# Last layer of a two-layer network on one core: biases inside the expert loop, rows added back on POOL, the end block by block

## The reference, cut to what matters

```python
x = x + _L1_ffn_ref(_layernorm(x, axis=-1), ...)

def _L1_ffn_ref(hidden_states, Wr, W1, b1, Wo, bo, gamma, beta):
    x = hidden_states.reshape(-1, H)
    expert_idx = jnp.argmax(jax.nn.softmax(x @ Wr.T, axis=-1), axis=-1)
    inter = jnp.zeros((x.shape[0], W1.shape[2]), dtype=x.dtype)
    for e in range(E):
        mask = (expert_idx == e)[:, None].astype(x.dtype)
        inter = inter + mask * jax.nn.gelu(x @ W1[e] + b1[e], approximate=False)
    y = inter @ Wo + bo + x
    mu = jnp.mean(y, axis=-1, keepdims=True)
    var = jnp.mean(jnp.square(y - mu), axis=-1, keepdims=True)
    return (y - mu) * jax.lax.rsqrt(var + LN_EPS) * gamma + beta
```

## Time and profile before

| | |
|---|---|
| median of 3 runs | 999.55 us (998.99 to 1000.77) |
| the profiled execution, its own time | 1001.5 us |
| its span, first to last instruction | 1000.2 us |
| busy over the span | PE 78%, DVE 68%, ACT 52%, POOL 24% |
| last part (from the barrier near 868 us) | 132 us |
| expert loop, first gather to last down copy | 896.4 to 973.6 us |
| behind the loop | 973.6 to 1000.2 us |

### The profile page before, as it was taken

The page is one execution under the profiler, slowest core; times in us unless marked ns, Lnnn a source line. Parts: engine busy times, 40 slices in busy tenths (PEclk is TensorE's granted clock), DMA queues, the critical chain, the costliest instruction groups (busy, mean ns, idle before and its releaser), DMA issues. The chain is left out here.

```text
span 1000.2 us, 17637 instructions
## 1 busy us (share of the span) xinstructions
PE 775.2 (78%) x6736; PEld 339.7 (34%) x6736; DVE 678.7 (68%) x1293; ACT 517.2 (52%) x994; POOL 237.2 (24%) x287
## 2 busy tenths in 40 slices
PE   4747998887623999970889899999999999628770
PEld 2315224663312666650411122222222222415650
DVE  5647997447676444438598899999999981573345
ACT  2563543265621333320516788888888887303342
POOL 0001101033205566634372200000000000026650
PEclk9967999998855999995956999999999999958995
DMA  3080000000070111114577221303300000051112
GB/s 105 0 168 3 2 1 13 5 4 1 0 291 31 40 43 43 41 31 143 175 156 185 77 48 30 75 6 72 76 2 3 2 2 2 17 224 43 42 33 87
DMA packets 40218, 58.06 MB, mean 58 GB/s; under 512 B 12025, under 2 KB 27393, under 8 KB 39369
## 3 DMA queue, kind: packets, MB, share of 16 engines
q1 hardware_dynamic: 36168, 48.82, 18.2%
q0 software_dynamic: 3968, 8.13, 3.1%
HBM read 37.99 MB, written 14.75 MB: 53 GB/s over the span
## 5 line engine op out<-in xcount | busy, mean ns | idle before, releaser
L867 DVE TENSOR_REDUCE arena<-psum 128x1 f32<-128x1024 f32 x256 | 301.0, 1216 | 26.5 <-PE psum L749 23.7
L963 ACT ACTIVATE arena<-psum 128x512 f32<-128x512 f32 x512 | 266.9, 604 | 53.1 <-PE psum L763 53.1
L749 PE MATMUL psum<-arena 56*128 56x512 bf16 x512 | 181.4, 413 | 8.4 <-DVE arena L867 4.7
L763 PE MATMUL psum<-arena 59*128 59x512 bf16 x512 | 157.8, 389 | 8.9 <-ACT arena L963 6.1
L774 PE MATMUL psum<-arena 128*32 128x512 f32 x1024 | 137.9, 611 | 8.7 <-issue 8.7
L763 PEld LDWEIGHTS psum<-arena 59*128 59x128 bf16 x512 | 37.8, 94 | 171.2 <-ACT arena L963 147.2
L437 POOL DMA_INDIRECT rows_y<-arena x62 | 62.8, 1012 | 64.0 <-DVE arena L392 61.3
L352 PEld LDWEIGHTS psum<-arena 128*128 128x128 f32 x496 | 62.9, 193 | 38.9 <-issue 25.5
L352 PE MATMUL psum<-arena 128*128 (+1 forms) x496 | 67.3, 279 | 10.7 <-ACT arena L416 10.7
L343 PE MATMUL psum<-arena 128*128 x124 | 68.0, 632 | 2.3 <-DVE arena L377 2.1
L432 POOL DMA_INDIRECT arena<-rows_x,arena x62 | 61.3, 989 | 34.7 <-issue 16.4
(11 more groups left out here) (292 smaller groups left out, 1138.7 us busy)
## 6 DMA issues: line engine op xcount, KB each, us to landing
arena<-scr_k SPq DMA_DIRECT2D x15, 448.0 KB
arena<-scr_q SPq DMA_DIRECT2D x15, 448.0 KB
arena<-in_f_up SPq DMA_DIRECT2D x1, 4096.0 KB, 13.0
arena<-rows_y SPq DMA_DIRECT2D x12, 256.0 KB, 4.8
scr_q<-arena SPq DMA_DIRECT2D x8, 384.0 KB, 3.7
arena<-in_f_down SPq DMA_DIRECT2D x1, 2048.0 KB, 17.9
rows_x<-xn SPq DMA_DIRECT2D x2, 1024.0 KB, 15.7
scr_k<-arena SPq DMA_DIRECT2D x8, 256.0 KB, 6.3
```

The costliest lines, as they stand in the source:

```text
L749: mm = pe.matmul(ps[:, bank + half, :], q[rows, k, h, (qh * 4 + qt) * P:(qh * 4 + qt + 1) * P], kk[rows, k, h, half * BLK:(half + 1) * BLK ...
L763: pe.matmul(ps[:, n % 3, :], kk[0:KA, k, h, kb * P:(kb + 1) * P], q[0:KA, k, h, qh * BLK:(qh + 1) * BLK], start=True, stop=True).then_inc( ...
L867: dve.tensor_reduce(mx[:, qh, h * 4 + qt:h * 4 + qt + 1], ps[:, bank:bank + 2, :].rearrange("p a b -> p (a b)"), X, ALU.max).then_inc(S("a ...
L963: act.activation(pt[:, (u % 3) * HG + h, :], ps[:, n % 3, :], ACT.Exp, scale=float(HD) ** -0.5).then_inc(S("a1_exp"), 1)
```

## The change

The bias bo and the bias beta are added block by block within the expert loop, behind L392 of steps 8, 11, 14 and 17: eight DVE instructions of 128x512 in place of two of 128x2048 outside it. The addition of the rows read back (L597) moves from DVE to POOL. Statistics, epsilon, root, reciprocal, offset and scaling are done for each block; DVE's order is statistics 0, 1, scales 0, statistics 2, scales 1, statistics 3, scales 2, scales 3, then the four finishing steps. The product with gamma moves to POOL for blocks 0 and 1, and stays on DVE for 2 and 3. What SP does is unchanged.

```diff
--- before.py
+++ after.py
@@ -364,7 +364,10 @@
                       start=True, stop=True).then_inc(again, 1)
 
 
-def experts_dve(c, name, top, gated):
+BIAS_STEPS = {8: 0, 11: 1, 14: 2, 17: 3}
+
+
+def experts_dve(c, name, top, gated, x=None):
     dve, ps, m, S = c.dve, c.psum, c.mem, c.sem
     n, xt, sg, h, y = tiles_of(top), m["e_xt"], m["e_sg"], m["e_h"], m["e_y"]
     stored = [S(f"{name}_stored{k}") for k in range(SLOTS)]
@@ -396,6 +399,10 @@
             dve.wait_ge(again, u.t + 1)
             dve.wait_ge(acted, u.t + 1)
             dve.tensor_tensor(h[:, u.pair, :], sg[:, u.pair, :], ps[:, 2 + u.pair, :], ALU.mult).then_inc(hidden, 1)
+        if not gated and s in BIAS_STEPS:
+            at = slice(BIAS_STEPS[s] * TPB, (BIAS_STEPS[s] + 1) * TPB)
+            for of, by in ((c.mem["xn"], m["f1_bo"]), (x, m["f1_beta"])):
+                c.own_dve.on(dve.tensor_tensor(of[:, at, :], of[:, at, :], by[:].unsqueeze(1).broadcast_to([P, TPB, D]), ALU.add))
 
 
 def experts_act(c, name, top, gated):
@@ -588,28 +595,45 @@
     route_dve(c, "f1", None, 1)
     y, bn, mv, rs, off, back = m["xn"], m["bn"], m["mv"], m["rs"], m["f1_off"], m["e_back"][:, 0]
     dve.wait_ge(S("f1_rows"), 16)
-    dve_step(c, dve.tensor_tensor(y[:], y[:], bc("f1_bo", NT), ALU.add))
-    experts_dve(c, "f1", 1, False)
-    dve_step(c, dve.tensor_tensor(x[:], x[:], bc("f1_beta", NT), ALU.add))
-    for n in range(NB):
-        dve.wait_ge(S(f"f1_back{n}0"), 16)
-        yb = y[:, n * TPB:(n + 1) * TPB, :]
-        dve_step(c, dve.tensor_tensor(yb, yb, back[:, n * TPB:(n + 1) * TPB, :], ALU.add))
+    experts_dve(c, "f1", 1, False, x)
+    m["f1_biased"] = own.n
+
+    def statistics(n):
+        dve.wait_ge(S("f1_summed"), n + 1)
         for t in range(n * TPB, (n + 1) * TPB):
             own.on(dve.bn_stats(bn[:, t, :], y[:, t, :]))
         dve.wait_ge(own.sem, own.n)
         for t in range(n * TPB, (n + 1) * TPB):
             own.on(dve.bn_aggr(mv[:, t, :], bn[:, t, :]))
-    dve.wait_ge(own.sem, own.n)
-    dve.tensor_scalar(rs[:], mv[:, :, 1], 1e-12, None, ALU.add).then_inc(S("f1_var"), 1)
-    dve.wait_ge(S("f1_root"), 1)
-    dve_step(c, dve.reciprocal(rs[:], rs[:]))
-    dve.scalar_tensor_tensor(off[:], mv[:, :, 0], -1.0, rs[:], ALU.mult, ALU.mult).then_inc(S("f1_off"), 1)
+        dve.wait_ge(own.sem, own.n)
+        at = slice(n * TPB, (n + 1) * TPB)
+        dve.tensor_scalar(rs[:, at], mv[:, at, 1], 1e-12, None, ALU.add).then_inc(S("f1_var"), 1)
+
+    def scales(n):
+        at = slice(n * TPB, (n + 1) * TPB)
+        dve.wait_ge(S("f1_root"), n + 1)
+        dve_step(c, dve.reciprocal(rs[:, at], rs[:, at]))
+        dve.scalar_tensor_tensor(off[:, at], mv[:, at, 0], -1.0, rs[:, at], ALU.mult, ALU.mult).then_inc(S("f1_off"), 1)
+
+    def finish(n):
+        at = slice(n * TPB, (n + 1) * TPB)
+        if n < 2:
+            dve.wait_ge(S("f1_gained"), n + 1)
+        else:
+            dve.wait_ge(S("f1_scaled"), n + 1)
+            dve_step(c, dve.tensor_tensor(back[:, at, :], back[:, at, :], bc("f1_gamma", TPB), ALU.mult))
+        dve.tensor_tensor(x[:, at, :], x[:, at, :], back[:, at, :], ALU.add).then_inc(S("f1_done"), 1)
+
+    statistics(0)
+    statistics(1)
+    scales(0)
+    statistics(2)
+    scales(1)
+    statistics(3)
+    scales(2)
+    scales(3)
     for n in range(NB):
-        at = slice(n * TPB, (n + 1) * TPB)
-        dve.wait_ge(S("f1_scaled"), n + 1)
-        dve_step(c, dve.tensor_tensor(back[:, at, :], back[:, at, :], bc("f1_gamma", TPB), ALU.mult))
-        dve.tensor_tensor(x[:, at, :], x[:, at, :], back[:, at, :], ALU.add).then_inc(S("f1_done"), 1)
+        finish(n)
 
 
 def ffn1_act(c):
@@ -617,13 +641,37 @@
     y, back, rs, off = m["xn"], m["e_back"][:, 0], m["rs"], m["f1_off"]
     norm_act(c, (6, 7), xnt_block(c))
     experts_act(c, "f1", 1, False)
-    act.wait_ge(S("f1_var"), 1)
-    act.activation(rs[:], rs[:], ACT.Sqrt).then_inc(S("f1_root"), 1)
-    act.wait_ge(S("f1_off"), 1)
-    for t in range(NT):
-        z = act.activation(back[:, t, :], y[:, t, :], ACT.Identity, scale=rs[:, t:t + 1], bias=off[:, t:t + 1])
-        if t % TPB == TPB - 1:
-            z.then_inc(S("f1_scaled"), 1)
+
+    def scaled(n):
+        act.wait_ge(S("f1_summed"), n + 1)
+        act.wait_ge(S("f1_off"), n + 1)
+        for t in range(n * TPB, (n + 1) * TPB):
+            z = act.activation(back[:, t, :], y[:, t, :], ACT.Identity, scale=rs[:, t:t + 1], bias=off[:, t:t + 1])
+        z.then_inc(S("f1_scaled"), 1)
+
+    for n in range(NB):
+        at = slice(n * TPB, (n + 1) * TPB)
+        act.wait_ge(S("f1_var"), n + 1)
+        act.activation(rs[:, at], rs[:, at], ACT.Sqrt).then_inc(S("f1_root"), 1)
+        if n:
+            scaled(n - 1)
+    scaled(NB - 1)
+
+
+def ffn1_pool(c):
+
+    pool, m, S = c.pool, c.mem, c.sem
+    y, back = m["xn"], m["e_back"][:, 0]
+    pool.wait_ge(c.own_dve.sem, m["f1_biased"])
+    for n in range(NB):
+        at = slice(n * TPB, (n + 1) * TPB)
+        pool.wait_ge(S(f"f1_back{n}0"), 16)
+        pool.tensor_tensor(y[:, at, :], y[:, at, :], back[:, at, :], ALU.add).then_inc(S("f1_summed"), 1)
+    for n in range(2):
+        at = slice(n * TPB, (n + 1) * TPB)
+        pool.wait_ge(S("f1_scaled"), n + 1)
+        pool.tensor_tensor(back[:, at, :], back[:, at, :], m["f1_gamma"][:].unsqueeze(1).broadcast_to([P, TPB, D]),
+                           ALU.mult).then_inc(S("f1_gained"), 1)
 
 
 def ffn1_pe(c):
@@ -641,6 +689,7 @@
     ffn1_act(c)
     route_pool(c, "f1", 1)
     experts_pool(c, "f1", 1, c.rows_x[1], c.rows_y[1])
+    ffn1_pool(c)
 
 
 def ffn1_layout(a, out):
```

## The result

| | before | after |
|---|---|---|
| median, same chip, 7 runs each | 1000.71 us (998.99 to 1004.07) | 995.37 us (993.26 to 999.39) |
| ratio | | 0.9947, 95% interval 0.9924 to 0.9970 |
| profiled execution / its span | 1001.5 / 1000.2 us | 993.54 / 992.0 us |

The kernel is faster by about 5.3 us (3.0 to 7.6); 3.3 were forecast. The forecast time, 996.2 us, lies closer to the measured 995.37 than the gains do, because it was set against the first three runs (median 999.55), and all seven of before have 1000.71. The two profiled spans differ by 8.2 us, but 2.77 of that lies ahead of L281 (which starts at 895.41 before, 892.64 after), in code that is the same in both. So I compare segments that start at L281. Each is the distance between two rows of the timeline.

A forecast was written before the change was run, and what follows sets the result against it. PE was taken to pace the last layer's expert loop, with one string of waits behind it. -1.1 - 1.8 + 1.0 - 1.4 = -3.3 us gave 996.2 us from the median 999.55; range 993.6 to 998.4.

The forecast's parts named there:

- First gather: Start of the last expert loop: with L591 gone, POOL's first gather falls from 2.33 to 1.19 us, -1.1 us.
- bound of -0.8: Worst case for the first gather: PE reaches full clock at the same absolute time, so part of the gain is lost.
- Last scatter: End of the loop: with L593 gone, POOL's last scatter falls from 2.76 to 0.97 us, -1.8 us.
- Eight additions: In the loop, steps 8, 11, 14, 17: pairs delay L384 and PE, 2 x 0.35 + 2 x 0.13 = +1.0 us.
- The end: Behind the read-back: sums on POOL and work by block end the last add at 996.4 instead of 997.8, -1.4 us.
- bound of -2.9: Lower bound for the end: DVE's own 12.1 us behind the first sum, last add at 994.9.
- The rule of the skill: Two-input DVE additions do not stall DMA issued from GpSimd; then -1.1 and -1.8 would not come, sum -0.4.
- The stops: Rival in the loop: PE stops once less (994.2 us, chance 0.12) or once more (998.2 us, chance 0.09).
- POOL holding off all of DVE: Rival at the end: statistics wait for POOL's fourth sum, +1.0 instead of -1.4, 998.6 us; chance 0.05.
- The long POOL instructions owed to something else: Rival: first gather and last scatter stay long, not owed to L591 and L593, 999.1 us; chance 0.05.
- Pairs against transfers: Slower rival in the loop: pairs and POOL's DMA instructions exclude each other, 2.35 us a pair, 1004.6 us; chance 0.06.

The follow-up runs named there:

- e1: Kernel before with the eight bias additions moved into the loop and the old end kept; 988.43 us beside 990.97 (ratio 0.9979).
- e2: Changed kernel with the two long additions put back outside the loop and no pairs, end by block kept; 989.40 us beside 990.97 (ratio 0.998).
- e12: Changed kernel with the end of e11 and the bias additions cut into 16 pairs of 128x128; 983.95 us, 0.9934 of the kernel before.
- e5: Changed kernel word for word again, on a chip where PE stops; 997.91 us beside 1001.69 for the kernel before (ratio 0.9967).
- e9: Changed kernel plus three unread DVE instructions (two-input addition, reduction, copy) in steps 19, 21, 23; 88.91 us from L281 to the end.
- e8: Changed kernel with twelve more addition pairs into unread memory, one pair in each of steps 4 to 19; loop 69.19 us.
- e3: Changed kernel with the four sums of read-back rows on DVE, POOL keeping only gamma of blocks 0 and 1; 988.58 us (ratio 0.9976).
- e7: Changed kernel with epsilon as the bias of ACT's square root and nothing else; 997.58 us (ratio 0.9942).
- e6: Changed kernel with the first sum on DVE and epsilon as the bias of ACT's root; 996.8 us (ratio 0.9950).
- e11: Changed kernel with sums 0 and 3 on DVE, epsilon in ACT's root, table loaded ahead, last two rows scaled on DVE; 985.33 us (ratio 0.9940).

## Why the prediction was right, and where its terms were off

- **First gather, -1.1 forecast.** The instruction did what was forecast: it took 1.05, not even layer 0's 1.19, and PE's first tile came 1.23 us sooner. e1 takes the addition away, e2 puts it back. But what this was worth was overrated, even beside the bound of -0.8. PE got its full clock no sooner behind L281, as the prediction had feared, and the first down copy came only 0.44 us earlier (0.55 in e1 against e2). Both traces with the long addition have PE at 1.2 GHz for 8.85 and 9.09 us of its loop, eleven of the twelve without it for 9.7 to 10.5; e12, with 7.77, shows that the rise is not fixed to L281 either.
- **Last scatter, -1.8 forecast, -1.80 measured.** Right in mechanism and size, and shown from both sides by e1 and e2.
- **Eight additions, +1.0 forecast.** The -0.07 of B doesn't measure them: it is +0.79 for the clock and -0.86 for stops that fell otherwise. The term was right behind a stop and too dear elsewhere. In an ordinary step I let a pair end 1.6 after L392's start; two in a row start 0.60 apart, so L387 followed after 1.40 instead of 1.35, 0.05 late and not 0.25, and e1's loop shows no cost (0.13 forecast). Two of the four pairs fell behind a stop (941.08 and 949.58); there L387 started 1.41 and 1.55 behind L395 instead of 0.77, so 0.64 and 0.78 late, and the loop did feel it. L387 and L380 came late, PE's next up product waited for L380 until 943.52, and the two steps behind 941.08 took 2.21 and 2.46 us. In before they take 1.95 and 2.34 behind the stop at 926.34. That is 0.38 for such a pair, where 0.35 was forecast. By these two prices the four pairs cost some 0.8 us here, an estimate; what they did to the later stops can't be told.
- **What made the sum come out.** With the terms as measured (-0.44 for the gather after what the clock took back, -1.80, +0.8, -2.33) the sum is -3.8, against -3.3 forecast and the 3.8 us of e5's medians. The overrated gather and the underrated end offset each other, which is luck. The other 1.7 of the -5.43 are stops that fell otherwise in this pair of traces.
- **The end, -1.4 forecast, -2.33 measured.** This term was too small by 0.9, within its bound of -2.9. The order and both kinds of hold were there, with one exchanged: the addition of epsilon (one input) was held for 0.94, which I had as free, and the first offset was not, as POOL was done by then. The two errors cancel, by luck: that offset ended at 981.00, 5.53 behind the landing of 975.47; I had 5.5. The last offset was held behind the second gamma product (1.02), as forecast. The rest is again the spacing of instructions in a row: sums 1.22 apart instead of 1.34, which brings the last offset to 10.31 behind the landing instead of 10.75, and six finishing operations in 3.85 us instead of 4.25.
- **The rule of the skill.** By the Trainium skill, "SBUF — State Buffer", section "Who interferes with whom", the two POOL terms would not come. They came, 3.0 us together; the measurement decides. The same section says that a tensor_scalar or a copy can hold or be held by GpSimd: by that, the trace agrees (L610, a tensor_scalar, took 1.11 for 0.17 in after; the copy held the scatter to 1.69 in e9).
- **The rivals.** The stops: behind the first down copy the loop was 0.86 shorter than before in after and 0.43 longer in e5, less than one stop of 2 us either way, so neither of those two came as a whole. POOL holding off all of DVE: the statistics took 0.87 beside it. The long POOL instructions owed to something else: e1 and e2. Pairs against transfers: e8. That the gain is one of chips with stops only: joining e1's A and C and B with e2's D on the chip without them gives 3.78 + 62.48 + 2.94 + 17.48 + 2.34 = 89.02, and the old ones 4.96 + 62.15 + 4.74 + 19.58 + 2.34 = 93.77, so 4.8 us there as against 5.4 here. e9, the changed kernel with three instructions more, measures 88.91 there.

## What to carry to other kernels

A long two-input DVE instruction (or an SBUF copy) that "costs nothing" because DVE is idle can hold up an indirect transfer on POOL at the moment when everything waits for it; look for POOL instructions that end 0.9 us after a DVE instruction, cut the DVE one into pieces and put them where the bound engine covers them. When work goes to POOL, list the small two-input and tensor_scalar instructions that DVE issues beside it: each waits for POOL's end, and the queue behind it too (e3: less work on DVE, and 0.9 us worse than with an idle POOL). Price instructions in a row by the distance of their starts, not by their durations. Time won ahead of PE's first product is only won if it is still there once the clock has risen: compare at the first product at full clock. And where the same code differs between two traces by more than the effect, as the read-back and the loop with stops do, cut the segment until it doesn't.

## What the runs showed of the hardware that I had not expected

- **The hold is on the start, and in one direction only.** A POOL transfer that starts beside a DVE addition ends 0.84 to 0.93 us behind that addition's end; a DVE addition that starts beside a running gather is not held (0.68 at 921.17). Of two additions in a row only the one beside which the transfer starts holds it (1.18 at 941.65 in after, 1.34 at 940.25 in e8).
- **An instruction on 128x4 values can cost 1.1 us,** if POOL adds beside it.
- **PE stops on some chips.** Before, after and e5 to e7 have loops of 72.9 to 73.95 us; the same loops elsewhere take 61.2 to 62.7. L395 then waits about 2 us longer for PE (2.56 at 925.82), and with twelve more pairs on DVE (e8) the loop was 4.6 us shorter. In before, after and e5 to e7 the granted clock also falls to 1.2 GHz once in mid-loop, for some 3.4 us (from 936.5 to 939.9 in before, from 927.3 to 930.8 in after); in the loops without stops, once risen, it stays at 2.4 GHz. The cause of the stops is open, and they are worth more than this whole change.
- **ACT's table load moves with the waits.** It lay beside the loop in after (at 967.91) and on the path, with its 1.28 us, in e6 and e7, where the root has another operand and the waits ahead of it are others. Which of the two moved it is not shown; a small root placed ahead of the wait (e11) brought the load back into the loop (960.93).
